# One fused attention, routing and expert stage: a new written order of the chunks, and the last chunk's routing woven with the shared groups

## The reference

```python
x = x + tanh(g_xattn[0]) * L0_xattn(layernorm(x), ctx, ...)
x = x + tanh(g_ffn[0])   * L0_ffn(layernorm(x), ...)     # the routed and the shared experts
x = x + tanh(g_xattn[1]) * L1_xattn(layernorm(x), ctx, ...)
x = x + tanh(g_ffn[1])   * L1_ffn(layernorm(x), ...)
# L0_ffn, per row: scores = sigmoid(x @ gate_w.T); top 4 of scores + gate_b;
# y = sum over those 4 of weight * (silu(x @ w1.T) * (x @ w3.T)) @ w2.T, plus the shared expert
```

## Time and profile before

| | |
|---|---|
| median of 3 runs | 1469.2 us (1464.93 to 1469.47) |
| profiled execution | 1465.75 us, its span 1464.0 us |
| PE, DVE, ACT, POOL busy | 77%, 69%, 45%, 34% of the span |
| chunks: first query product to the last add | 34.7 to 370.1 us |
| routed groups: SP's first and last load | 429.6 to 652.2 us |

### The profile page before, as it was taken

The page is one execution under the profiler, slowest core; times in us unless marked ns, Lnnn a source line. Parts: engine busy times, 40 slices in busy tenths (PEclk is TensorE's granted clock), DMA queues, the critical chain, the costliest instruction groups (busy, mean ns, idle before and its releaser), DMA issues. The chain is left out here.

```text
span 1464.0 us, 25236 instructions
## 1 busy us (share of the span) xinstructions
PE 1126.2 (77%) x8327; PEld 606.6 (41%) x8327; DVE 1007.6 (69%) x1863; ACT 664.6 (45%) x1401; POOL 503.9 (34%) x576
## 2 busy tenths in 40 slices
PE   3786777775487777781877589999999999988858
PEld 2343344434375666660444123333333333331646
DVE  3677887875564544444996778888888888860665
ACT  1454344453232322220333066777776777775430
POOL 1226655666716766673000611112111111111110
PEclk7898879877699999995889589999999999995989
DMA  6011222222888888874796411211112111100003
GB/s 194 22 36 59 73 93 82 86 94 75 235 198 170 172 167 181 172 154 183 228 286 213 132 41 49 68 41 40 40 41 62 56 40 40 41 2 0 1 1 115
DMA packets 203515, 145.81 MB, mean 100 GB/s; under 512 B 134392, under 2 KB 178427, under 8 KB 203402
## 3 DMA queue, kind: packets, MB, share of 16 engines
q1 hardware_dynamic: 180778, 102.76, 28.1%
q0 software_dynamic: 13728, 34.64, 7.0%
q10 hardware_dynamic: 8896, 6.90, 1.6%
HBM read 53.19 MB, written 69.75 MB: 84 GB/s over the span
## 5 line engine op out<-in xcount | busy, mean ns | idle before, releaser
L1788 DVE TENSOR_REDUCE small<-ps 128x2 f32<-128x960 f32 (+6 forms) x384 | 379.0, 1041 | 56.7 <-PE ps L1843 56.5
L1767 ACT ACTIVATE region<-ps 128x512 f32<-128x512 f32 (+5 forms) x768 | 343.1, 533 | 107.9 <-PE ps L1857 106.5
L1738 POOL TENSOR_SCALAR_AFFINE_SELECT region<-region 128x512 f32<-128x512 f32 (+2 forms) x160 | 87.3, 546 | 425.7 <-ACT region L1767 425.7
L1857 PE MATMUL ps<-region 50*128 50x512 f16 (+5 forms) x896 | 197.7, 330 | 27.2 <-ACT region L1767 23.9
L1933 PE MATMUL ps<-region 128*32 128x512 f32 (+5 forms) x1792 | 191.6, 501 | 2.5 <-POOL region L1738 1.9
L703 POOL DMA_INDIRECT result_rows<-region,small x158 | 157.9, 999 | 99.2 <-DVE region L1047 58.4
L1218 PE MATMUL ps<-region 128*128 128x256 f16 x1140 | 149.8, 285 | 53.8 <-DMA region<-expert_rows 45.8
L1843 PE MATMUL ps<-region 48*128 48x480 f16 (+6 forms) x896 | 141.6, 334 | 13.5 <-DVE small L1788 11.3
L1218 PEld LDWEIGHTS ps<-region 128*128 (+1 forms) x1140 | 110.0, 102 | 88.9 <-issue 67.5
L1857 PEld LDWEIGHTS ps<-region 50*128 50x128 f16 (+1 forms) x896 | 54.4, 95 | 209.7 <-ACT region L1767 195.1
L1028 DVE SCALAR_TENSOR_TENSOR region<-ps,region 128x256 f32<-128x256 f32 x95 | 40.3, 424 | 128.9 <-ACT region L810 123.6
(11 more groups left out here) (219 smaller groups left out, 1735.3 us busy)
## 6 DMA issues: line engine op xcount, KB each, us to landing
region<-result_rows SPq DMA_DIRECT2D x16, 1024.0 KB, 6.8
region<-v_parts SPq DMA_DIRECT2D x16, 576.0 KB, 4.0
v_parts<-region SPq DMA_DIRECT2D x14, 576.0 KB, 6.9
region<-k_parts SPq DMA_DIRECT2D x96, 68.0 KB, 2.2
region<-q_parts SPq DMA_DIRECT2D x96, 64.0 KB, 2.1
k_parts<-region SPq DMA_DIRECT2D x16, 272.0 KB, 4.4
x_sb<-in_x ACTq DMA_DIRECT2D x8, 512.0 KB, 9.0
region<-in_w13T SPq DMA_DIRECT2D x16, 256.0 KB, 3.2
```

The lines of the kernel that those rows point to most:

```text
L1738: nc.gpsimd.affine_select(out=t, in_=t, compare_op=ALU.is_ge, fill=0.0, base=r0, pattern=[[0, G], [1, w]], channel_multiplier=-1).then_inc ...
L1767: nc.scalar.activation(dst, src, ACT.Exp, scale=SCALE).then_inc(s_exp, 1)
L1788: nc.vector.tensor_reduce(nmp[:, qt, :, p0:p0 + np_, place], s_pair(n + first)[:, :, 0:np_ * nk] .rearrange("p e (h k) -> p e h k", h=np_) ...
L1857: ins = nc.tensor.matmul(o, k_of(rr, tbuf)[:, pair, kt * P:kt * P + rows], q_of(rr, tbuf)[:, pair, q0:q0 + nq], start=True, stop=True)
```

## The change

**Chunks.** The attention norm of chunk c+2 no longer runs at the end of pass c and into its successor: its statistics move on DVE from behind `slots` to the head of the pass, directly behind those of the routing norm; `nmu`, `nmr`, the variance and the scale get two buffers each, so that two norms can be under way. PE transposes the next chunk's inputs (x0, x1) in pass c, ahead of the outputs, and ACT moves them there; the queries of chunk c+1 then need nothing but these. `add` moves on DVE ahead of the last two row sums, `high` on ACT to the head of the pass, `ranks` on PE from before the values to behind the last scores. POOL sends 4 of a chunk's 16 transfers in the pass that routes it and 12 in the next (before: 8 and 8), with both norms' scales ahead of ten of them.

**Last chunk.** `targets` and `slots` of chunk 6 move behind the last add. The first shared groups are started before the last chunk's norm: their steps stand between its transposes, logits and ranks on PE, between its norm, moves and tanh on ACT, and between `rows_low` and `choose` on DVE. SP loads shared groups 4 and 5 ahead of the tables, ACT fills 8 tails, one ahead of each of groups 6 to 13, and SP the other 8.

**Banks.** Gate and up of a group share one bank (g % 3), shared groups have one result bank (3), so that `group_down(g)` waits for the add of group g-1, and routed groups use banks 4 and 5 for results.

The core of the diff:

```diff
-            order = queries(0)
+            order = inputs(0) + queries(0) + inputs(1)
             for c in range(CHUNKS):
-                order += queries(c + 1) if c < LAST else []
+                order += queries(c + 1)
                 order += probs_of(c, range(2)) + rows_of(c - 1) + probs_of(c, range(2, 4)) + logits_of(c - 1)
-                order += probs_of(c, range(4, 8)) + ranks_of(c - 1) + outputs_of(c)
+                order += probs_of(c, range(4, 8)) + values_of(c)
+                if c < LAST:
+                    order += ranks_of(c - 1) + inputs(c + 2) + outputs_of(c)
+                else:
+                    order += outputs_of(c) + ranks_of(c - 1)
...
-            ACT_TAILS = 5
+            ACT_TAILS = 8
+            TAILS_FROM = 6
...
+            def result(g):
+                return ps[:, DEEP if g < FIRSTS else RING + g % 2, :]
...
+                for g in range(G_BUFS, TAILS_FROM):
+                    shared_rows(g)
                 store_dense(LAST)
                 for dst, src in ((w_sb[:, :, 0:D], wq1), (w_sb[:, :, D:3 * D], wkv1), (c_sb, ctxT)):
                     sp.dma_start(dst, src.rearrange("(k p) n -> p k n", p=P)).then_inc(s_win, 16)
                 sp.wait_ge(s_tabs, 1)
-                for g in range(G_BUFS, FIRSTS):
-                    if ACT_TAILS + g - G_BUFS < E:
-                        fill_tail(sp, ACT_TAILS + g - G_BUFS)
+                for g in range(TAILS_FROM, FIRSTS):
+                    if ACT_TAILS + g - TAILS_FROM < E:
+                        fill_tail(sp, ACT_TAILS + g - TAILS_FROM)
                     shared_rows(g)
...
+                    if n >= 2:
+                        pool.wait_ge(s_xn, (n - 1) * TC)
+                    nc.gpsimd.tensor_tensor(rstds[:, n % 2, :], vars_[:, n % 2, :], half[:], ALU.pow).then_inc(s_pow, 1)
...
+                EARLY, LATE = 4, 6
                 for c in range(CHUNKS):
                     if c:
                         rstd_of(2, c - 1)
                     if c >= 2:
-                        send(c - 2, 8, 16)
+                        send(c - 2, EARLY, LATE)
+                    if c + 2 < CHUNKS:
+                        rstd_of(1, c + 2)
+                    if c >= 2:
+                        send(c - 2, LATE, 16)
                     if c < LAST:
                         normalise(c + 1, range(2))
-                    if c and c < LAST:
-                        send(c - 1, 0, 2)
-                    if c + 2 < CHUNKS:
-                        rstd_of(1, c + 2)
-                    if c and c < LAST:
-                        send(c - 1, 2, 8)
-                    if c < LAST:
+                        if c:
+                            send(c - 1, 0, EARLY)
                         normalise(c + 1, range(2, TC))
...
-                send(LAST - 1, 0, 4)
                 rstd_of(2, LAST)
-                send(LAST - 1, 4, 16)
+                send(LAST - 1, 0, 16)
...
                 for c in range(CHUNKS):
+                    for expert in experts_beside(c):
+                        high(*expert)
                     if c < LAST:
                         move_queries(c + 1)
                     if c:
                         normalised(2, c - 1)
-                    for expert in experts_beside(c):
-                        high(*expert)
...
                     move_probs(c, range(4, 8))
-                    move_outputs(c)
                     if c + 2 < CHUNKS:
                         if c:
                             act.wait_ge(s_lo, c)
                         normalised(1, c + 2)
+                    move_outputs(c)
                     if c < LAST:
                         exp(c + 1, 2)
+                    if c + 2 < CHUNKS:
+                        move_inputs(c + 2)
+                    if c < LAST:
                         exp(c + 1, 3)
+                for g in range(2):
+                    silu(g)
+                    hidden_high(g)
                 act.wait_ge(s_lo, LAST)
                 normalised(2, LAST)
                 rows_high(LAST)
+                silu(2)
+                hidden_high(2)
                 move_rows(LAST)
+                silu(3)
+                hidden_high(3)
                 tanh(LAST)
...
+                for g in range(4, ALL_GROUPS):
+                    if g == TAILS_FROM:
+                        act.wait_ge(s_fill, 1)
+                        act.wait_ge(s_tabs, 1)
+                    if TAILS_FROM <= g < TAILS_FROM + ACT_TAILS:
+                        fill_tail(act, g - TAILS_FROM)
                     silu(g)
+                    hidden_high(g)
...
                 for c in range(CHUNKS):
                     more = c < LAST
                     if c:
-                        dve.wait_ge(s_dve, moved(turn[c - 1, "o1"]))
-                        statistics(2, c - 1)
+                        second(c - 1)
+                    if c + 2 < CHUNKS:
+                        statistics(1, c + 2)
...
+                    if not more:
+                        break
+                    if c:
                         targets(c - 1)
-                    if more:
-                        shift(c + 1, 2)
-                        row_sum(c + 1, 1)
+                    shift(c + 1, 2)
+                    row_sum(c + 1, 1)
                     if c:
                         slots(c - 1)
-                    if c + 2 < CHUNKS:
-                        statistics(1, c + 2)
-                    if more:
-                        shift(c + 1, 3)
-                        row_sum(c + 1, 2)
-                        row_sum(c + 1, 3)
+                    shift(c + 1, 3)
                     add(c)
-                dve.wait_ge(s_dve, moved(turn[LAST, "o1"]))
-                statistics(2, LAST)
-                rows_low(LAST)
-                choose(LAST)
-                targets(LAST)
-                slots(LAST)
-                tables()
...
-                for g in range(DEEP - 1):
-                    group_hidden(g)
-                    group_hidden_low(g)
-                for g in range(ALL_GROUPS):
+                    row_sum(c + 1, 2)
+                    row_sum(c + 1, 3)
+                add(LAST)
+                second(LAST)
+                targets(LAST - 1)
+                slots(LAST - 1)
+                def group_step(g):
...
+                for g in range(DEEP - 1):
+                    group_hidden(g)
+                    group_hidden_low(g)
+                rows_low(LAST)
+                group_step(0)
+                group_step(1)
+                choose(LAST)
+                targets(LAST)
+                slots(LAST)
+                tables()
+                for g in range(2, ALL_GROUPS):
+                    group_step(g)
...
+                                ins = nc.tensor.matmul(ps[:, g % DEEP, half_ * GROUP:(half_ + 1) * GROUP], w, xgT[:, g % G_BUFS, part, kh, :],
...
+                def group_down(g, e):
+                    eng.wait_ge(s_ghl, g + 1)
+                    if 0 < g < FIRSTS:
+                        eng.wait_ge(s_yout, g)
+                    elif g >= FIRSTS + 2:
+                        eng.wait_ge(s_yout, g - 1)
+                    elif g >= FIRSTS:
+                        eng.wait_ge(s_act, moved(turn[LAST, "lg"]))
+                        eng.wait_ge(s_dve, moved(turn[LAST, "count"]))
...
-                    if c:
-                        ranks(c - 1)
                     values(c)
                     if more:
                         scores(c + 1, 3)
+                        if c:
+                            ranks(c - 1)
+                    if c + 2 < CHUNKS:
+                        inputs_of(c + 2)
                     outputs(c)
...
+                ranks(LAST - 1)
...
+                experts = []
+                for g in range(DEEP - 1):
+                    experts.append(expert(g))
+                    group_gate_up(g, experts[-1])
+                group_step(0)
+                transposed(LAST, 2, ("r0", "r1"))
+                group_step(1)
+                logits(LAST)
+                group_step(2)
+                ranks(LAST)
+                wait_free(LAST, "count")
+                nc.tensor.matmul(slot(LAST, "count")[:, 0:E], onesb[:], counts[:, CHUNKS, :], start=True,
+                                 stop=True).then_inc(s_full, 1)
+                for g in range(3, ALL_GROUPS):
+                    group_step(g)
```

188 lines of the change are left out of this document (91 added, 97 removed).

## The result

The changed kernel takes 1424.9 us in the median of four executions (1416.99 to 1428.74) against 1468.1: a ratio of 0.9702, interval 0.9657 to 0.9747. A second set of runs on another chip gave 1424.4 and 0.9729 (0.9698 to 0.9761). It is faster, by 43 us where 54 were forecast.

What follows compares the result with a forecast made beforehand. A loop through several engines was taken to set the passes, SP's loads the routed stage. 1465.75 - 41.4 (six passes) - 6 (pass 0) - 7 (pass 7) + 1 (tail) = 1412.3; stated as median 1415, range 1399 to 1440.

Steps and rivals of the forecast that it cites:

- The loop: Middle passes: last row sum, POOL's tiles, PE's transposes and scores, DVE's shifts to row sums; 2.4 + 5.5 + 26.6 = 34.5 us.
- the low clock: PE's transposes and first scores after its pause: 5.5 us taken at the lower level, 2.9 at full clock.
- 33.0 and 34.5: Length of a middle pass: 33.0 us if PE runs at full clock, 34.5 at the lower level; 41.4 before.
- the ring: PE's four result banks in the passes: every turn followed was said to be moved out in time.
- holds as a rival: POOL's first tile holds DVE in targets, up to 1.9 us a pass: passes of 36.4, total 1427; chance 0.20.
- the rule that spoke against the change: GpSimd contends with VectorE instructions having two SBUF inputs, so products of targets would be held wherever a tile falls.
- all three waits: In a pass: DVE's 2.65 and 4.43 us, PE's 3.10 for the add; all said to lose their cause.
- Pass 7: Last pass, add to add: norm starts at about 4, 20 more behind it, 24 against 30.9; 7 us saved.
- The tail: Last add to first routed load: 60.5 us against 59.5 before, +1, ends -4 and +8.
- The step of 3.0 us a tail: ACT's tails strung behind silu 6 to 13: 3.0 us each, the eighth issued at 55.6 after the last add.
- Routed stage: Paced by SP's 79 loads, one each 2.85 us; moves as a block with its first load, 0 change.
- Shared bank: One result bank for shared groups: 0 cost, up to 12 us if all 16 adds of 0.74 stood bare.

Runs made afterwards that it cites:

- e11: The changed kernel run again unaltered on another chip: median 1424.4 us, ratio 0.9729 to the kernel before.
- e1: Changed kernel with two more POOL transfers ahead of a pass's first tile (EARLY 4 to 2, LATE 6 to 4): 1419.5 us, ratio 0.9686 to the kernel before.
- e7: Changed kernel with each query product computed twice into the same bank: 1414.1 us, ratio 0.9705 to the kernel before.
- e9: e8 with each query product computed twice: 1402.4 us, ratio 0.9566 to the kernel before.
- e2: Changed kernel with the add behind the last two row sums again: 1415.0 us, ratio 0.9664 to the kernel before.
- e10: Changed kernel with queries behind the add, slots ahead of the row sum, transfers split, last chunk's routing ahead of all shared groups: 1396.5 us, ratio 0.9526.
- e12: e10 with the last chunk's routing woven into the shared groups again: 1401.1 us, ratio 0.9566 to the kernel before.
- e8: Changed kernel with slots first, add behind row sums, EARLY and LATE as in e1, transfers split, routing ahead of shared groups: 1407.2 us, ratio 0.9638.
- e5: Changed kernel with PE starting a pass's queries only behind the add again: 1414.7 us, ratio 0.9710 to the kernel before.
- e3: Changed kernel with slots ahead of the row sum that releases POOL's second tile: 1420.5 us, ratio 0.9710 to the kernel before.

## Why the prediction was nearly right

**The loop was the right one.** In the short pass above, counted from the end of the last row sum, POOL's tile ends at 2.5 (forecast 2.4), the first shift starts at 6.8 (7.9 at the low clock, 6.4 by DVE's own path at the full one) and shifts to row sums take 26.7 (26.6). That pass is 33.5, between the two values of 33.0 and 34.5. In the long pass the counts are 8.1 and 28.6: the start at the low clock as worked out, and 2 us more behind it, the hold. One turn of the ring is not free, as the prediction had it: the second half of the outputs (L1186) waits 1.0 to 3.1 us in passes 1 to 5 for `slots` to leave the bank of the ranks. DVE shows no wait ahead of its adds for it; what it does to the queries behind it was not tried.

**The step that was mis-sized: holds as a rival with a chance of its own.** The forecast let every pass be 34.5 and the rival every pass 36.4. It is neither all nor none: three or four passes of six have the hold and are 35.9 to 36.8, the others 33.5 to 34.2. The mean of 35.1 (35.6 in e11) costs 3.9 us against the forecast. A pass at the low clock without the hold, for which the 34.5 stands, hardly comes up: from 0.92 us of waiting on, the hold comes with it. I had not seen that the two unknowns hang together: the low clock delays the first shift by a microsecond, and this decides whether `targets` meets the tile (e1, which moves the tile, and e7 and e9, which raise the clock). The Trainium skill (GPSIMD Engine Reference, Specifications) names instructions with two SBUF inputs as contending with GpSimd; the trace agrees in L968, 0.23 against 2.21 us, so the rule that spoke against the change decided half of the passes.

**The cuts were credited wrongly.** The text let all three waits be cut by the three edits. Undone one by one, only the high halves were needed (11.5 us to the last add). With the queries behind the add the six passes are 10.3 us shorter in sum; with the add behind the row sums they are 2.2 shorter, which I can't tell from nothing. Either edit alone kept the 3.10 us wait of the earlier trace rows out of the loop; both undone together was not run. The early queries bring a pause on PE, which stays when the add moves back (e2's granted clock is 0.86 to 0.90 in passes 2 to 6). The doubled scale buffers, which let the attention norm start early, were not tried alone. So of the 37.5 us of the six passes the runs assign some 11 to the high halves and leave the rest undivided.

**Pass 7: 27.3, not 24.** "Now POOL has only the last tile (2.4) and a scale ahead of the norm" mixed two zero points. The 2.4 count from the end of the last row sum, and the add now ends 2.8 us before that; POOL's two tiles start 1.5 us behind the add, the scale is done at 302.4, and the norm starts 7.3 us behind the add instead of 4. These 3.3 us have the size of the whole miss, since the 20 us behind the norm came as forecast. That is in part luck, as the clock is not in that term: the changed kernel's granted clock in pass 7 is 0.62. In e1 the norm starts at the same 7.3 us, the granted clock is 0.74, and the add ends 16.0 us behind the norm. PE's logits of that pass, in the changed kernel and in e1:

```profile
307.55 3.57 PE L1196 MATMUL ps<-small 128*128 128x16 f32 x16
...
305.72 1.93 PE L1196 MATMUL ps<-small 128*128 128x16 f32 x16
```

All runs with EARLY = 2 have this shorter pass (23.3 in e1, e10 and e12; 20.5 and 20.1 in e8 and e9, where the add of pass 6 stands later, against 24.3 in e2). Why their clock is higher there stays open.

**The tail: 63.0, not 60.5.** Tanh at 15.7 (16.0), SP's first tail at 24.5 (24.5) and ACT's at 33.2 (33) came as worked out; the wait of 13.12 us behind DVE's tables is there. The step of 3.0 us a tail was too small: 3.66 over seven, since the last two rounds waited 3.63 and 4.93 us for products whose shared rows SP loaded late (PE waited 3.25 and 3.07 us for these loads). The eighth tail thus left at 58.9 instead of 55.6.

**Routed stage: no cost**, as said. **Shared bank: one wait that the prediction put at nothing.** It looked at a middle step; behind the tables PE's fourth down product waits 9.01 us for the add of the group before, which DVE writes only behind the tables:

```profile
353.74 1.44 PE L1242 MATMUL ps<-region 128*128 128x256 f16 x6 [9.01 <-DVE x_sb L1039]
```

ACT's second round of the tails then waits 2.77 us for the products behind it. Whether this is part of the tail's 3.6 us is not shown: no run gives the bank back.

**The median.** The median lies 8 us above the profiled execution, the fastest of four; the forecast was for the median. Stage and layer 1 both vary: e11's profile, at 1422.4, has one held pass more and 4.1 us more in layer 1.

## What to carry to other kernels

When several waits of a loop are cut at once, ask of each edit whether the others have already taken its cause away: here two edits did one job, and by e5's trace the stage is shorter without the early queries. Give an engine's pause to work that nobody waits for; a start-up at the lower clock is free there and dear in front of the loop's next step. And two small uncertain costs that meet in time (a late start, a neighbour's tile) are one case, not two.

## What the runs showed of the hardware

A hold between POOL and DVE ends with POOL's instruction, however short DVE's own: 0.2 us became 2.21 or 2.45, and 0.43 became 3.92 beside two tiles in a row. It also strikes a scaling of 128 x 4 numbers with one input (0.17 to 2.62 us in e3). A reduction over the probabilities (1.21) and a shift, which reads PSUM (1.22), kept their lengths beside the tile at 216.23.

Doubling PE's query work raised the granted clock of passes 2 and 3 from 0.86 to 1.00 and 0.95 (e7), and that of pass 5 from 0.90 to 1.00 (e9 against e8); the passes became shorter by it.
